# A tile's scatters wait, besides its slots, for the cross query products of the tile two behind it

## Chip, cores, metric

The kernel runs on one core of a Trainium2 chip. The metric is the device time of one execution in microseconds (us); lower is better. The engines are named as in the profile: PE (TensorE), PEld (its weight loads), DVE (VectorE), ACT (ScalarE), POOL (GpSimd) and SP (SyncE).

## What is computed

One decoder layer over 32 sequences of 128 tokens with 512 features: causal self attention with rotary positions, cross attention to a context with int8-like rounding, and a mixture of 64 experts. What is rounded, and what the experts take, is the part that matters here:

```python
def _qdq(x):
    s = jnp.maximum(jnp.max(jnp.abs(x), axis=-1, keepdims=True) / 127.0, 1e-08)
    return jnp.clip(jnp.round(x / s), -127.0, 127.0) * s
...
q = _qdq(x) @ _qdq(wq).T + bq                    # cross query products
...
out = _qdq(o) @ _qdq(wp).T + bp                  # cross attention's output
...
pos = (jnp.cumsum(onehot, axis=0) * onehot).sum(-1) - 1
valid = pos < CAP
dest = jnp.where(valid, slot_expert * CAP + pos, E * CAP)
buf = jnp.zeros((E * CAP + 1, h), xf.dtype).at[dest].set(xf[slot_token])
...
x = x + _L0_attn_ref(_layernorm(x, axis=-1), ...)
x = x + _L0_xattn_ref(_layernorm(x, axis=-1), ctx_2048, ...)
x = x + _L0_ffn_ref(_layernorm(x, axis=-1), ...)
```

Each token goes to 8 of the 64 experts, and each expert takes at most 128 tokens, in the order of the tokens. A token that comes too late for an expert is left out of it.

## The kernel before

**Two stages.** First all 32 sequences pass through both attentions and the router; one sequence of 128 tokens is one tile. Each tile's normed rows are written to a buffer in HBM, `routed`, at the slots of their experts. Then, once all rows are there, the 64 experts run one after the other. The change touches the first stage alone.

**A software pipeline written out by hand.** Each engine runs its own list of steps in its own program order, and `body(cur)` is one pass of it: `Fori(7, B + 1)` makes 26 such passes, and the passes before and behind it are written out. In one pass five tiles are under way at different steps: queries, keys and values of tile `cur - 1`, self attention of `cur - 2`, the cross queries and scores of `cur - 3`, the end of the cross attention of `cur - 4`, and the routing of `cur - 5`. An engine never goes past a step that waits: whatever stands behind it in its list waits as well. Steps of different engines meet through semaphores; `reached(eng, semaphore, m, per, j)` makes an engine wait until the j-th of a tile's `per` signals has come for tile m.

**POOL's list in one pass**, in order: `ctx_hi` (L1829) and `ctx_lo` (L1836), which split the context of tile `cur - 3` in two parts for PE; between them `bias_first_sum` (L1832); `number_tokens` (L1843); `cross_power`, `turned_x_hi`, `turned_x_lo`, `self_power`; then `scatter(cur - 5)` (L1867), then `ffn_power(cur - 4)` (L1822) and `bias_residual(cur - 2)` (L1877). `scatter` issues eight indirect DMAs of 128 rows, one for each of a token's eight experts; rows without a place are skipped. It waits for `d_r2`, DVE's signal that the slot numbers are ready (the last instruction of `slot_numbers` is at L1424).

**The steps around it.** On DVE `find_slots` is followed at once by the cross attention's norm and rounding of tile `cur - 3`. On PE `cross_queries(cur - 3)` multiplies the rounded rows with the rounded weights (`project_int8`, L534, semaphore `p_cq`; `cross_output` shares the line). It stands just behind `turn_probs_1` (`turn_probs`, L556, semaphore `p_pT`). ACT picks both up: `copy_probs_1` (L1022 into `probsT`), then `scale_cross_queries` (L1124 into `cq`, a part of `wide_b`). PE turns the scaled queries (L510 on `wide_b`), multiplies `cross_output` (DVE's `second_sum`, L1384, takes it), turns the probabilities 2 and 0, and makes `cross_scores` (L549) and `turn_probs_3`. DVE's `cross_max_0` and `cross_max_1` (L1341) take the scores, `ffn_rsqrt` (L1318 to L1322, L1481) takes POOL's `ffn_power`, and behind it stand `cross_max_2`, `cross_max_3`, `att_lo`, `rotate` and `first_sum`. ACT's `copy_probs_3` takes `turn_probs_3`, then come `cross_exp_0` and `att_hi` (L1022 into `attT_hi`); PE needs `att_hi` for the products `output_b` and `output_a` (L528 on `w_o`).

Of the kernel before, what the change touches and what calls it, by code (L numbers as in the profile page):

```python
# [66 lines left out]
def nth(ordinal, per, j):  # L67

    return (ordinal - 1) * per + j


def until(eng, semaphore, value):

    if not isinstance(value, int) or value > 0:
        eng.wait_ge(semaphore, value)
# [7 lines left out]
def reached(eng, semaphore, m, per, j):  # L83

    if isinstance(m, int):
        if m < 1:
            return
        m = min(m, B)
    until(eng, semaphore, nth(m, per, j))
# [7 lines left out]
def apart(eng):  # L97


    eng.nop(nofuse=True)  # L100


def layer(nc, x, xT_in, ctxT_in, qT_w, kT_w, vT_w, oT_w, xkT_w, xvT_w, xq_w, xp_w, biases, vb, xkb, xvb, ob, xbq, xbp, routerT,
# [7 lines left out]
    def sem(name):  # L111
        return st.enter_context(nc.semaphore(name))

    with st:
# [89 lines left out]
        def spare(m):  # L204

            return isinstance(m, int) and m == B - 1

        def row_of(m):

            return empty_row if spare(m) else row  # L210
# [5 lines left out]
        def slots_of(m):  # L216

            return slots_spare if spare(m) else slots
# [40 lines left out]
        p_q8T, p_cq, p_cqT = sem("pe_xq8T"), sem("pe_cq"), sem("pe_cqT")  # L259
# [1559 lines left out]
        def _(pool):  # L1819
# [42 lines left out]

            def scatter(m, first=0, end=TOPK):
                reached(pool, d_r2, m, 6, 6)
                apart(pool)
                for k in range(first, end):
                    pool.indirect_dma_start(routed, bass.IndirectOffsetOnAxis(ap=slots_of(m)[:, k:k + 1], axis=0), row_of(m)[:, :], None,  # L1867
                                            bounds_check=SLOTS - 1,
                                            oob_is_err=False).then_inc(s_scatter_spare if spare(m) else s_scatter, 16)
# [9 lines left out]
            def body(cur, split=True):  # L1879
                if has(cur - 3):  # L1880
                    ctx_hi(cur - 3)
                if has(cur - 4):
                    bias_first_sum(cur - 4)
                if has(cur - 3):
                    ctx_lo(cur - 3)
                if has(cur - 5):
                    number_tokens(cur - 5)
                if has(cur - 3):
                    cross_power(cur - 3)
                if has(cur - 1) and split:  # L1890
                    turned_x_hi(cur - 1)
                if has(cur - 1) and split:
                    turned_x_lo(cur - 1)
                if has(cur - 1):
                    self_power(cur - 1)
                if has(cur - 5):
                    scatter(cur - 5)
                if has(cur - 4):
                    ffn_power(cur - 4)
                if has(cur - 2):  # L1900
                    bias_residual(cur - 2)
# [33 lines left out]
            number_tokens(B - 1)  # L1935
            number_tokens(B)
            scatter(B - 1, 0, 2)
            ffn_power(B)
            scatter(B - 1, 2, TOPK)
            scatter(B)  # L1940
            pool.wait_ge(s_scatter, 16 * TOPK * (B - 1))
# [69 lines left out]
```

## Time and profile before

| | |
|---|---|
| median of 3 runs | 1680.09 us (1678.44 to 1685.43) |
| the profiled execution | 1680.71 us, its span 1678.9 us |
| busy share of the span | PE 85%, DVE 71%, PEld 64%, ACT 56%, POOL 43% |
| mean granted TensorE clock | 0.938 of full speed |

A timeline row gives the start, the duration, the engine, the source line, the operation, what it writes and reads, and how many instructions are merged in the row; in brackets stands the engine's idle time before it and what ended it. `remote` there means that the wait ended on a signal that the profile can't put down to an instruction that had just finished. A row of the waits gives the total, the number of times and the longest.

### The profile page before, as it was taken

To read this page: it belongs to the slowest core of one execution; us is meant where nothing else is said; L and a number is where in the kernel's file an instruction comes from. 1 tells how busy PE (TensorE), PEld (TensorE's weight loads), DVE (VectorE), ACT (ScalarE), POOL (GpSimd) and SP (SyncE) were. 2 spreads that over 40 slices of the span, in tenths; PEclk is the share of its full clock that TensorE was granted. 3 is DMA by queue.
4 is the path that set the end of the run, shared out by engine and by line. 5 is a ranking of instruction groups with operands and counts; after the bars stand their busy time and mean duration, and the time that the engine had idled before them with its cause. 6 is when DMAs were issued, how large, how long until landed. Compare 5 with 4: busy or idle time off the path is not lost.

```text
span 1678.9 us, 36380 instructions
## 1 busy us (share of the span) xinstructions
PE 1421.1 (85%) x11243; PEld 1069.3 (64%) x11276; DVE 1189.6 (71%) x3054; ACT 940.6 (56%) x3309; POOL 727.1 (43%) x718
## 2 busy tenths in 40 slices
PE   5499889999988999889899999989864888888895
PEld 3377667777666777666677777767643655555564
DVE  3778878888887888888788888888862444444453
ACT  2367676676666666666666766666742333333342
POOL 1113434444443444445444344444433454445565
PEclk8699999999999999999999999999976999999997
DMA  6765322222211111111111001110464999999964
GB/s 187 296 220 205 136 94 100 92 92 95 100 46 36 38 32 31 31 56 32 31 38 31 31 31 56 31 31 26 161 227 153 282 280 276 279 263 282 280 103 52
DMA packets 164530, 204.33 MB, mean 122 GB/s; under 512 B 40246, under 2 KB 122422, under 8 KB 164481
## 3 DMA queue, kind: packets, MB, share of 16 engines
q1 hardware_dynamic: 125568, 165.86, 30.0%
q0 software_dynamic: 38912, 37.87, 11.1%
q8 instruction: 24, 0.39, 0.1%
q14 instruction: 26, 0.21, 0.0%
HBM read 136.19 MB, written 130.29 MB: 159 GB/s over the span
## 4 chain that ended last, share of the span: by engine, by line
PE 37%; DMA 19%; issue 12%; ACT 10%; DVE 8%; another core or an unknown queue 7%; POOL 1%; POOLq 0%; DVEq 0%; SPq 0%
DMA out<-x,slots 19%; PE bank L528 18%; ACT probs L1028 7%; PE bank L556 6%; PE bank L510 3%; PE bank L563 3%; PE bank L534 2%; PE bank L549 2%; PE bank L569 1%; ACT wide_b L1124 1%; ACT wide_b L1099 1%; DVE small L1308 1%; DVE small L1341 1%; POOL routed L1867 1%
## 5 line engine op out<-in xcount | busy, mean ns | idle before, releaser
L1028 ACT ACTIVATE probs<-bank,small 128x128 f32<-128x128 f32 x1024 | 363.5, 389 | 88.1 <-issue 50.0
L1867 POOL DMA_INDIRECT routed<-row,slots x248 | 253.7, 1023 | 126.7 <-issue 77.4
L1822 POOL TENSOR_TENSOR small<-small,half 128x1 f32<-128x1 f32 x96 | 54.4, 567 | 544.5 <-DVE small L1313 544.5
L1950 POOL DMA_INDIRECT out<-x,slots x128 | 199.0, 1554 | 195.8 <-DMA out<-x,slots 148.4
L1022 ACT ACTIVATE probsT<-bank 128x512 f32<-128x512 f32 x254 | 144.2, 609 | 214.4 <-remote 116.3
L1028 ACT ACTIVATION_READ_ACCUMULATOR probs<-bank,small 128x1 f32 x1024 | 234.6, 229 | 0.0
L1341 DVE TENSOR_REDUCE small<-bank 128x4 f32<-128x512 f32 x256 | 166.4, 682 | 23.0 <-PE bank L549 17.6
L556 PE MATMUL bank<-idf,probs 128*128 128x128 f32 x1024 | 164.8, 300 | 8.5 <-ACT probs L1028 8.4
L556 PEld LDWEIGHTS bank<-idf,probs 128*128 128x128 f32 x1024 | 134.1, 156 | 42.0 <-ACT probs L1028 13.2
L1777 DVE TENSOR_SCALAR slots<-pairs 128x1 uint32<-128x1 f32 x128 | 13.7, 149 | 184.0 <-DMA out<-x,slots 180.3
L1271 ACT ACTIVATE xn<-bank 128x192 f32<-128x192 f32 x64 | 21.3, 333 | 148.2 <-PE bank L968 133.0
L1384 DVE SCALAR_TENSOR_TENSOR x<-bank,small,xp_row 128x512 f32<-128x512 f32 x32 | 24.0, 751 | 110.1 <-PE bank L534 105.7
L968 PE MATMUL bank<-w_gate_up,x_in 128*128 128x384 f32 x256 | 96.0, 522 | 0.5 <-issue 0.5
L1350 DVE TENSOR_TENSOR probs<-probs,small 128x512 f32<-128x512 f32 x128 | 88.8, 693 | 4.4
L968 PE MATMUL bank<-w_gate_up,x_res 128*128 128x384 f32 x256 | 91.3, 501 | 0.0
L510 PE MATMUL bank<-idf,wide_b 128*128 128x128 f32 x128 | 23.1, 309 | 76.9 <-ACT wide_b L1124 76.9
L510 PEld LDWEIGHTS bank<-idf,wide_b 128*128 128x128 f32 x128 | 14.8, 149 | 89.1 <-ACT wide_b L1124 88.7
L968 PEld LDWEIGHTS bank<-w_gate_up,x_in 128*128 128x128 f32 x256 | 49.6, 204 | 30.5 <-issue 7.7
L968 PEld LDWEIGHTS bank<-w_gate_up,x_res 128*128 128x128 f32 x256 | 47.7, 196 | 27.2 <-issue 3.3
L528 PE MATMUL bank<-w_q_hi,xT_hi 128*128 128x512 f32 x128 | 57.8, 451 | 7.8 <-issue 7.8
L528 PE MATMUL bank<-w_o_hi,attT_hi 128*128 128x512 f32 x132 | 54.5, 413 | 11.6 <-DVE attT_lo L1697 10.6
L1783 DVE TENSOR_SCALAR x<-bank,pairs 128x256 f32<-128x256 f32 x128 | 55.5, 476 | 0.0
(250 smaller groups left out, 3974.5 us busy)
## 6 DMA issues: line engine op xcount, KB each, us to landing
w_gate_up<-in_w_gate SPq DMA_DIRECT2D x128, 192.0 KB
w_gate_up<-in_w_up SPq DMA_DIRECT2D x128, 192.0 KB
w_down<-in_w_down SPq DMA_DIRECT2D x128, 192.0 KB
routed<-empty_row SPq DMA_DIRECT2D x16, 1280.0 KB, 11.3
x_in<-in_x SPq DMA_DIRECT2D x32, 256.0 KB
xn<-in_xT_in SPq DMA_DIRECT2D x32, 256.0 KB
ctx_sb<-in_ctxT_in SPq DMA_DIRECT2D x32, 256.0 KB
x_res<-in_x SPq DMA_DIRECT2D x32, 256.0 KB
```

Of the source, the lines that this page charges most:

```text
L510: last = pe.transpose(bank[:, b, t * P:(t + 1) * P], src[:, t * P:(t + 1) * P], idf[:, :])
L528: done = pe.matmul(bank[:, b, :], lhsT, rhs, start=first and k == 0, stop=last and k == len(steps) - 1)
L556: last = pe.transpose(bank[:, b, j * P:(j + 1) * P], probs[:, g, j * P:(j + 1) * P], idf[:, :])
L968: last = pe.matmul(bank[:, 2 + k % 2, 0:2 * F], rowsT[k % 2][:, t * P:(t + 1) * P], w_gu[k][:, :, t, :], start=(t == 0), stop=(t == KT - 1))
L1022: act.activation(dst, src, ACT.Copy).then_inc(done, 1)
L1028: last = act.activation(probs[:, g, j * P:(j + 1) * P], bank[:, b, j * P:(j + 1) * P], ACT.Exp, bias=negated[:, h:h + 1], **({"accum_out": ...
L1341: dve.tensor_reduce(negated[:, g * GH:(g + 1) * GH], bank[:, b, :].rearrange("p (j k) -> p j k", j=GH), AX_X, ALU.max, negate=True).then_i ...
L1350: dve.tensor_tensor(heads, heads, own.unsqueeze(2).to_broadcast([P, GH, P]), ALU.mult).then_inc(d_norm, 1)
L1783: last = dve.tensor_scalar(scaled_y[k % 2][:, cols], bank[:, half_bank(c, k), cols], share[k % NROWS], None, ALU.mult)
L1822: pool.tensor_tensor(c["r0"], c["v"], half[:, :], ALU.pow).then_inc(g_pow[kind], 1)
L1867: pool.indirect_dma_start(routed, bass.IndirectOffsetOnAxis(ap=slots_of(m)[:, k:k + 1], axis=0), row_of(m)[:, :], None, bounds_check=SLOTS ...
L1950: pool.indirect_dma_start(out.rearrange("b p (h c) -> (b p h) c", h=2), bass.IndirectOffsetOnAxis(ap=place_of[k % 2][:, half_:half_ + 1], ...
```

## The change

One line is added to POOL's `scatter`:

```diff
             def scatter(m, first=0, end=TOPK):
                 reached(pool, d_r2, m, 6, 6)
+                reached(pool, p_cq, m + 2, 1, 1)
                 apart(pool)
                 for k in range(first, end):
```

`scatter` is called with `m = cur - 5`, so the new wait is for the cross query products of tile `cur - 3`: those that PE makes in the same pass. For the last tiles the tile number is cut to 32, whose products are there by then. No work is added or taken away.

## Rows read from the trace of the kernel before

**Rows 1.** The waits: engine, what, releaser; us in total, times, longest.

```profile
ACT probsT L1022 <- remote: 116.3, 26, 4.6
```

**Rows 2.** Timeline of PE in two passes.

```profile
721.07 0.66 PE L556 MATMUL bank<-idf,probs 128*128 128x128 f32 x4
721.78 0.81 PE L534 MATMUL bank<-xq_wT,xq8T 128*128 128x512 bf16 x3
...
728.13 0.65 PE L510 MATMUL bank<-idf,wide_b 128*128 128x128 f32 x4 [2.90 <-ACT wide_b L1124]
...
759.01 0.81 PE L534 MATMUL bank<-xq_wT,xq8T 128*128 128x512 bf16 x3
```

**Rows 3.** Timeline of ACT in the same passes.

```profile
726.90 0.60 ACT L1022 ACTIVATE probsT<-bank 128x512 f32<-128x512 f32 x1 [4.48 <-remote]
...
736.76 0.60 ACT L1022 ACTIVATE attT_hi<-bank 128x512 fp32r<-128x512 f32 x1
...
772.44 0.61 ACT L1022 ACTIVATE attT_hi<-bank 128x512 fp32r<-128x512 f32 x1
```

**Rows 4.** Timeline of POOL: scatters of several passes, and what follows in one.

```profile
162.78 1.25 POOL L1867 DMA_INDIRECT routed<-row,slots  x1 [1.56 <-issue]
...
715.21 1.09 POOL L1867 DMA_INDIRECT routed<-row,slots  x1 [1.38 <-DVE chosen_before L1424]
...
724.54 0.98 POOL L1867 DMA_INDIRECT routed<-row,slots  x1 [0.30 <-issue]
...
752.44 1.10 POOL L1867 DMA_INDIRECT routed<-row,slots  x1 [1.38 <-DVE chosen_before L1424]
...
770.46 0.57 POOL L1822 TENSOR_TENSOR small<-small,half 128x1 f32<-128x1 f32 x1 [7.72 <-DVE small L1313]
...
787.92 1.10 POOL L1867 DMA_INDIRECT routed<-row,slots  x1 [1.38 <-DVE chosen_before L1424]
...
1156.26 1.10 POOL L1867 DMA_INDIRECT routed<-row,slots  x1 [1.38 <-DVE chosen_before L1424]
```

**Rows 5.** Timeline of DVE in the same passes.

```profile
714.16 0.19 DVE L1424 TENSOR_TENSOR chosen_before<-chosen_before,chosen 128x64 bf16<-128x64 bf16 x1
...
735.40 0.27 DVE L1318 TENSOR_SCALAR small<-small 128x1 f32<-128x1 f32 x1
...
771.53 0.27 DVE L1318 TENSOR_SCALAR small<-small 128x1 f32<-128x1 f32 x1
```

**Rows 6.** Two stretches by window; behind POOL's count stands the granted clock.

```profile
729.48:732.89 3.41, 3.41 (x13) 2.70 (x11) 2.86 (x6) 2.85 (x10) 0.00 (x0) 0.50 0.15 59
...
1210.76:1214.17 3.41, 2.84 (x7) 2.26 (x8) 3.37 (x4) 2.92 (x13) 2.45 (x3) 0.50 0.00 0
```

**Rows 7.** The pass at 1198 to 1213 us: POOL, PE, ACT and DVE.

```profile
1199.80 0.97 POOL L1867 DMA_INDIRECT routed<-row,slots  x1 [6.22 <-issue]
...
1207.03 0.97 POOL L1867 DMA_INDIRECT routed<-row,slots  x1 [0.30 <-issue]
...
1198.96 0.81 PE L534 MATMUL bank<-xq_wT,xq8T 128*128 128x512 bf16 x3
...
1205.04 0.66 PE L556 MATMUL bank<-idf,probs 128*128 128x128 f32 x4
...
1208.80 0.60 ACT L1022 ACTIVATE probsT<-bank 128x512 f32<-128x512 f32 x1 [3.93 <-remote]
...
1210.66 0.62 ACT L1022 ACTIVATE attT_hi<-bank 128x512 fp32r<-128x512 f32 x1
...
1207.96 1.39 DVE L1341 TENSOR_REDUCE small<-bank 128x4 f32<-128x512 f32 x2 [2.29 <-remote]
...
1209.75 3.13 DVE L1322 TENSOR_TENSOR small<-small 128x1 f32<-128x1 f32 x1
```

**Rows 8.** The pass at 677 to 693 us: POOL and DVE.

```profile
682.70 0.99 POOL L1867 DMA_INDIRECT routed<-row,slots  x1 [4.10 <-issue]
...
693.00 0.75 DVE L1384 SCALAR_TENSOR_TENSOR x<-bank,small,xp_row 128x512 f32<-128x512 f32 x1 [4.41 <-remote]
```

## The prediction, made before the change was run

> **What bounds the kernel now.** I read the page first: PE is busy for 85% of the span, so the question is what its idle time waits for. The waits give one answer that stands out: ACT's copy of turned probabilities waited 26 times, about 4.5 us each, 116.3 us in all [rows 1]. Then I read the timelines of PE, ACT and POOL side by side over one pass. The transposes that this copy waits for ended at 721.07 + 0.66 = 721.73, but ACT started at 726.90 [rows 2, 3]. So PE's result was there 5.2 us before ACT learned of it. POOL's eight scatters run in just this time: the first starts at 715.21, the last ends at 724.54 + 0.98 = 725.52 [rows 4]. ACT is let go 1.38 us after that end. I read this as follows: while POOL issues scatters back to back, PE's signals come late, and they come in a bunch shortly after the last one. The cause inside the chip I can't see; the timing I can.
>
> Through the late signal PE goes idle for 2.90 us [rows 2], and in most passes a stretch at granted clock 0.50 (the 1.2 GHz level) follows at once [rows 6]. A pass with that stretch lasts 752.44 - 715.21 = 37.23 us, one without it 787.92 - 752.44 = 35.48 us, and the mean over 27 passes is (1156.26 - 162.78) / 27 = 36.80 us [rows 4]. So 75% of the passes are long ones ((36.80 - 35.48) / 1.75).
>
> **What the change removes and adds.** Let P be the end of the cross query products: 722.59 in the long pass, 759.82 in the short one [rows 2]. Now the slots are ready 714.16 + 0.19 = 714.35 [rows 5], 8.2 us before P, so the new wait does hold the scatters. `turn_probs_1` and the products themselves then signal with no scatter under way. The 4.5 us wait of the copy goes.
>
> What is late next? I follow one tile from P.
> - P to the first scatter: 715.21 - 714.35 = 0.86 us, what POOL takes now from its releaser to the first scatter [rows 4, 5].
> - Eight scatters: 725.52 - 715.21 = 10.31 us [rows 4].
> - End of the scatters to the late signals: 1.38 us in the pass above, 1208.80 - (1207.03 + 0.97) = 0.80 us in the pass of [rows 7].
> - From the copy of `turn_probs_3` to the end of `att_hi`: 1210.66 + 0.62 - 1208.80 = 2.48 us [rows 7].
>
> So `att_hi`, on which PE's output products hang, ends 14.45 to 15.03 us after P. Today it ends 736.76 + 0.60 - 722.59 = 14.77 us after P in a long pass and 772.44 + 0.61 - 759.82 = 13.23 us in a short one [rows 2, 3]; with 75% long passes that is 14.39 us. The direct cost is 0.06 to 0.64 us a tile; I take 0.3, between the two release times.
>
> Why do I believe that `turn_probs_3` will be held? The trace of before holds one pass in which scatters start right at P: products end at 1198.96 + 0.81 = 1199.77, six scatters start at 1199.80. `turn_probs_3` ended at 1205.70, ACT took it at 1208.80 after 3.93 us of waiting, and DVE's first cross maxima waited 2.29 us as well [rows 7]. After the change every pass looks like this, with eight scatters in place of six.
>
> Two costs come on top.
> - **The clock.** In the pass of [rows 7] PE had little to do from the cross scores until `att_hi`, and the clock then fell to 0.50 for 3.41 us, right in the output products [rows 6]. Today's drop lies ahead of `att_hi` and is inside the 14.77. A drop behind it costs between 0 (DVE's chain is late anyway) and 1.75 us (the difference of a long and a short pass). I take half, 0.9: behind `att_hi` both PE's products and DVE's `att_lo`, `rotate` and `first_sum` stand in front of the next pass, and no row tells which ends last then.
> - **DVE beside POOL.** `ffn_power` stands behind the scatters on POOL, so DVE's `ffn_rsqrt` now runs just as POOL does `bias_residual`, `ctx_hi`, `bias_first_sum` and `ctx_lo` without a break. In the pass of [rows 7] the tiny L1322 took 3.13 us there; its neighbour L1318 of the same size takes 0.27 [rows 5]. That is 0 to 2.86 us a tile; I take 0.4, since it is spent on DVE, beside PE's drop, and the rows show one such case.
>
> The Trainium skill speaks against the change here: GPSIMD Engine Reference, Key points, says that GpSimd shares its SBUF interfaces with VectorE, which contends in instructions with two SBUF inputs, as L1322 is one. The 3.13 us agrees. The page gives no price, so the sum by it would hold this term with an unknown size; the sum by the row holds at most 2.86 us.
>
> What else is queued behind the wait: `ffn_power`, `bias_residual` and the next pass's `ctx_hi`. POOL waits 7.72 us ahead of `ffn_power` today [rows 4], which is nearly all the delay of 0.86 + 8.2 us. No SP load waits for a step that is newly held. The added wait itself is an instruction or two on a POOL that is idle then: nothing.
>
> **The sum.** 0.3 + 0.9 + 0.4 = 1.6 us a tile. 27 passes from 162.78 to 1156.26 are hit; the pass behind them has its scatters there already, and the expert stage is untouched. 27 x 1.6 = 43 us. On the profiled execution's 1680.7 us that is **1724 us**; the median of the runs is 0.6 us lower, which I neglect. Bounds: 27 x 0.06 = 2 us below, and 27 x (0.64 + 1.75 + 0.4) = 75 us above, 1682 to 1756. If the whole 2.86 us of L1322 were to show, it would take the place of the clock's cost and give 27 x (0.64 + 2.86) = 95 us; I count that as unlikely.
>
> **Rivals.**
> - *Faster: PE's signals get through, and POOL alone sets the pace.* It needs `turn_probs_3` and the cross scores to signal within about the first half of the scatters. Then DVE's `ffn_rsqrt` still waits for `ffn_power`: P + 0.86 + 10.31 + (771.53 - 770.46 = 1.07) = P + 12.24 us [rows 4, 5]. In a short pass it starts at P + 11.71, and the rest of a short pass is 35.48 - 11.71 = 23.77 us. The pass becomes 36.01 us, 0.79 less than the mean; 27 x 0.79 = 21 us, 1659 us. For it: the held signals of [rows 7] come 5.24 us and more behind the first scatter (1205.04 against 1199.80), and those of [rows 2] 5.9 us behind it, so steps that are quicker than this could get ahead of the hold. Against it: in [rows 7] the steps were not quicker, with the same work in front of them.
> - *Far slower: `cross_output` is held too.* In the pass of [rows 8] POOL paused 4.10 us after its first scatter, the rest ran later than usual, and `second_sum` waited 4.41 us for `remote`. If each tile pays that: 27 x 4.41 = 119 us, 1800 us. Against it: `cross_output` stands on PE ahead of the cross scores, so it signals earlier than 5.24 us into the scatters.
> - *No change.* The wait of the copy is replaced by one of equal length, and the clock drop costs what it does today: 27 x 0.06 = 2 us, 1682 us.
> - *The wait does nothing.* Excluded by the 8.2 us above.
>
> **How the numbers follow.** Forecast (slower, 1724 us) 0.70; faster 0.18; no change 0.07; far slower 0.05. The range leaves out the far slower case and a part of the ends: 1658 to 1756 us. The forecast's own range is 1682 to 1756. A measurement of this kernel tells about 0.5% (8 us) from no change: slower 0.73 (the forecast without its low end, and the far slower case), same 0.09, faster 0.18.
>
> **What would show it.** In the changed kernel's timeline the copy behind `turn_probs_1` should wait under 1 us for PE; the first scatter should start about 0.9 us after the cross query products; ACT's copy into `probsT` ahead of `cross_exp_0`, or DVE's L1341 on the cross scores, should wait for `remote` until about 1 us after the last scatter; stretches at 0.50 should start behind that wait; and the pass should last about 38.4 us. If none of these waits is there and the pass lasts 36 us, the first rival is right. If L1384 waits for `remote`, it is the second. I would be wrong at the root if PE's signals were late with no scatter under way.

## The result, and the profile after

The changed kernel takes 1767.00 us in the median of three runs (1763.18 to 1767.14), the kernel before 1679.26 us beside it: a ratio of 1.0508, with a 95% interval of 1.0471 to 1.0546. A fourth run of the changed kernel, at 3395.22 us a slow one, is left out. The change is slower, by 88 us in place of the forecast 43, and 11 us above the upper end of the range. The direction and the signs by which I wanted to know the mechanism are there; the size is not.

The waits of the changed kernel come first (engine, line waited for: us in all, times, longest):

```profile
POOL routed L1868 <- PE bank L534: 279.1, 29, 12.9
ACT probsT L1022 <- remote: 189.4, 28, 7.2
...
DVE small L1341 <- remote: 154.7, 29, 6.5
```

The scatters now wait for the cross query products (the first row). The row `probsT <- remote` of [rows 1] stands here again under the same name, but grown from 116.3 us in 26 waits to 189.4 us in 28, and it is another copy: the one of `turn_probs_3`. DVE's maxima of the cross scores wait in the same way. One pass shows it (timelines; start, us, engine, operation, and in brackets the idle time before it with what ended that):

```profile
758.09 0.81 PE L534 MATMUL bank<-xq_wT,xq8T 128*128 128x512 bf16 x3
...
764.34 1.17 PE L549 MATMUL bank<-wide_b 32*128 32x128 f32 x32
765.44 0.66 PE L556 MATMUL bank<-idf,probs 128*128 128x128 f32 x4
...
772.36 1.51 PE L563 MATMUL bank<-probsT,v_sb 128*32 128x128 f32 x24 [4.18 <-ACT probsT L1022]
...
781.81 1.00 PE L569 MATMUL bank<-router_w,x3T 128*128 128x64 f32 x8
...
758.54 0.67 ACT L1022 ACTIVATE probsT<-bank 128x512 f32<-128x512 f32 x1
...
771.71 0.60 ACT L1022 ACTIVATE probsT<-bank 128x512 f32<-128x512 f32 x1 [6.83 <-remote]
...
773.93 0.60 ACT L1022 ACTIVATE attT_hi<-bank 128x512 fp32r<-128x512 f32 x1 [0.18 <-PE bank L563]
...
759.75 1.10 POOL L1868 DMA_INDIRECT routed<-row,slots  x1 [9.51 <-PE bank L534]
...
769.35 0.97 POOL L1868 DMA_INDIRECT routed<-row,slots  x1 [0.30 <-issue]
770.33 0.59 POOL L1822 TENSOR_TENSOR small<-small,half 128x1 f32<-128x1 f32 x1
...
773.89 1.27 POOL L1836 TENSOR_TENSOR cT_lo<-ctx_sb,cT_hi 128x512 fp32r<-128x512 f32 x1
...
771.53 1.29 DVE L1341 TENSOR_REDUCE small<-bank 128x4 f32<-128x512 f32 x2 [5.42 <-remote]
...
773.22 1.96 DVE L1322 TENSOR_TENSOR small<-small 128x1 f32<-128x1 f32 x1
...
782.04 0.68 DVE L1506 TENSOR_TENSOR x<-bank,x_res 128x512 f32<-128x512 f32 x1
782.86 0.22 DVE L1510 TENSOR_REDUCE small<-bank 128x1 f32<-128x64 f32 x1
```

The copy behind `turn_probs_1` (758.54) no longer waits: the 4.48 us of [rows 3] are gone. The cross scores ended at 764.34 + 1.17 = 765.51 and `turn_probs_3` at 766.10, but DVE and ACT learned of it at 771.53 and 771.71, just over 1 us behind the end of the last scatter (769.35 + 0.97 = 770.32). `ffn_power`, for which POOL waited 7.72 us in [rows 4], follows the scatters at once. Behind the stall the clock is at its lower level, as in [rows 6], but now in the attention and value products (windows; us, then busy time of PE, PEld, DVE, ACT and POOL, then granted clock, DMA share and GB/s):

```profile
772.41:773.80 1.39, 1.39 (x25) 0.94 (x25) 1.32 (x4) 1.34 (x8) 1.39 (x2) 0.50 0.00 0
773.80:777.21 3.41, 3.41 (x12) 2.71 (x9) 3.37 (x6) 3.27 (x15) 1.72 (x3) 0.53 0.00 0
```

To see where the time lies I take the starts of `router_max` (L1510), one in each pass. After:

```profile
191.91 0.22 DVE L1510 TENSOR_REDUCE small<-bank 128x1 f32<-128x64 f32 x1 [0.58 <-PE bank L569]
...
1253.36 0.22 DVE L1510 TENSOR_REDUCE small<-bank 128x1 f32<-128x64 f32 x1 [0.58 <-PE bank L569]
...
1333.52 0.20 DVE L1510 TENSOR_REDUCE small<-bank 128x1 f32<-128x64 f32 x1
```

Before, the same three, and two from the middle that are used further down:

```profile
189.58 0.23 DVE L1510 TENSOR_REDUCE small<-bank 128x1 f32<-128x64 f32 x1
...
744.43 0.21 DVE L1510 TENSOR_REDUCE small<-bank 128x1 f32<-128x64 f32 x1
...
779.91 0.23 DVE L1510 TENSOR_REDUCE small<-bank 128x1 f32<-128x64 f32 x1
...
1184.29 0.22 DVE L1510 TENSOR_REDUCE small<-bank 128x1 f32<-128x64 f32 x1
...
1251.81 0.20 DVE L1510 TENSOR_REDUCE small<-bank 128x1 f32<-128x64 f32 x1
```

Between the first two rows lie 27 passes: (1253.36 - 191.91) / 27 = 39.31 us each, against (1184.29 - 189.58) / 27 = 36.84 us. That is 27 x 2.47 = 66.7 us. The two passes up to the last of these rows take 80.16 against 67.52 us: 12.6 us more. Ahead of them the span has grown by 191.91 - 189.58 = 2.3 us, behind them by 0.8 us. The sum, 82.4 us, is the difference of the spans (1761.4 and 1678.9 us); the profiled run is the quickest of the three, so it shows 82 of the 88 us.

### The profile page after: what moved, and what is told of

Same layout as the page of the kernel before. It is cut to its first block, busy times and chain, and to the rows that moved or that the text cites. A ratio compares the mean times of both kernels' runs of the same rounds, so it can differ in the third digit from the quotient of the medians.

```text
span 1761.4 us, 36380 instructions
## 1 busy us (share of the span) xinstructions
PE 1453.7 (83%) x11243; PEld 1088.9 (62%) x11276; DVE 1221.3 (69%) x3054; ACT 943.9 (54%) x3309; POOL 730.9 (41%) x718
## 4 chain that ended last, share of the span: by engine, by line
DVE 31%; DMA 18%; PE 16%; issue 15%; another core or an unknown queue 10%; ACT 4%; POOL 2%; DVEq 1%; POOLq 0%; SPq 0%
DMA out<-x,slots 18%; PE bank L528 10%; DVE small L1341 4%; DVE small L1308 3%; DVE small L1331 2%; DVE small L1322 2%; DVE chosen L1405 2%; PE bank L563 1%; ACT probs L1028 1%; POOL routed L1868 1%; PE bank L556 1%; ACT probsT L1022 1%; DVE wide_a L1377 1%; ACT wide_b L1137 1%
## 5 line engine op out<-in xcount | busy, mean ns | idle before, releaser
L1868 POOL DMA_INDIRECT routed<-row,slots x248 | 258.0, 1040 | 366.0 <-PE bank L534 279.1
L1341 DVE TENSOR_REDUCE small<-bank 128x4 f32<-128x512 f32 x256 | 166.5, 682 | 162.7 <-remote 154.7
L1022 ACT ACTIVATE probsT<-bank 128x512 f32<-128x512 f32 x254 | 145.2, 617 | 231.0 <-remote 189.4
L1028 ACT ACTIVATION_READ_ACCUMULATOR probs<-bank,small 128x1 f32 x1024 | 228.0, 223 | 0.0
L563 PE MATMUL bank<-probsT,v_sb 128*32 128x128 f32 x1024 | 74.4, 374 | 115.5 <-ACT probsT L1022 96.0
L556 PE MATMUL bank<-idf,probs 128*128 128x128 f32 x1024 | 150.2, 280 | 14.5 <-ACT probs L1028 11.0
L556 PEld LDWEIGHTS bank<-idf,probs 128*128 128x128 f32 x1024 | 119.1, 143 | 45.1 <-ACT probs L1028 17.0
L563 PEld LDWEIGHTS bank<-probsT,v_sb 128*32 128x32 f32 x1024 | 41.2, 145 | 146.3 <-ACT probsT L1022 108.9
L528 PE MATMUL bank<-w_v_hi,xT_hi 128*128 128x512 f32 x128 | 75.6, 591 | 0.0
L1322 DVE TENSOR_TENSOR small<-small 128x1 f32<-128x1 f32 x96 | 69.7, 726 | 3.3
L528 PE MATMUL bank<-w_v_lo,xT_hi 128*128 128x512 f32 x128 | 68.8, 537 | 0.4 <-issue 0.4
```

The source lines that it names most:

```text
L528: done = pe.matmul(bank[:, b, :], lhsT, rhs, start=first and k == 0, stop=last and k == len(steps) - 1)
L556: last = pe.transpose(bank[:, b, j * P:(j + 1) * P], probs[:, g, j * P:(j + 1) * P], idf[:, :])
L563: last = pe.matmul(bank[i * DH:(i + 1) * DH, b, g * P:(g + 1) * P], values[:, h * DH:(h + 1) * DH], probsT[:, g, i * P:(i + 1) * P], start ...
L1022: act.activation(dst, src, ACT.Copy).then_inc(done, 1)
L1028: last = act.activation(probs[:, g, j * P:(j + 1) * P], bank[:, b, j * P:(j + 1) * P], ACT.Exp, bias=negated[:, h:h + 1], **({"accum_out": ...
L1322: dve.tensor_tensor(c["r"], c["u"], c["r0"], ALU.mult).then_inc(s, 1)
```

## The experiments

Theory A, from the prediction: scatters that POOL issues back to back hold PE's signals, and the added wait moves the hold from `turn_probs_1` to the cross scores and `turn_probs_3`. Rival B: POOL's own order (`ffn_power` behind the scatters) sets the pace. Rival C: the late signals belong to a place in PE's program. Rival D: the low clock behind the stall is the larger part. All ratios below are to the kernel before on the same chip; "a pass" is the mean of the 27 passes as above, in the profiled run. Before it is 36.84 us, after the change 39.31. Of each edit the lines that matter are shown.

### Four scatters in place of eight, before and after

```diff
-                for k in range(first, end):
+                for k in range(first, min(end, 4)):
```

> The kernel before with four of eight scatters for each tile; the rows of places 5 to 8 are left out, so the output lacks their shares. A: the run ends 5.1 us after its start, ahead of the end of turn_probs_1, so the copy no longer waits 4.5 us, 1530 to 1600 us. B: POOL waits 7.7 us ahead of ffn_power already, so shorter scatters bring nothing: 1680 us. C: 1680 us.

> The changed kernel with four of eight scatters for each tile; the rows of places 5 to 8 are left out, so the output lacks their shares. A: the run ends at P + 6.0 us and the cross scores end at P + 7.2 us, so the waits of 6.8 us (copy into probsT) and 5.4 us (L1341) vanish, a pass lasts 32 to 35 us, 1550 to 1630 us. B: ffn_power comes 5.1 us sooner, at most 27 x 5.1 = 139 us less than 1763, if all of that shows; half of it gives 1690. C: 1763 us, as POOL is not part of it.

Measured: 1535.60 us without the added wait (ratio 0.9118, 0.9094 to 0.9142; a pass 32.06 us) and 1543.79 us with it (0.9164, 0.9138 to 0.9189; a pass 32.01 us). Of the waits for `remote` only single ones are left, where the kernel before had 26 and the changed one 28 and 29. C falls. The hold costs the kernel before 36.84 - 32.06 = 4.8 us a pass, and with runs this short the added wait costs nothing a pass; the 8 us between the two kernels lie in the last passes.

### POOL as busy as before, but no scatter

```diff
-                for k in range(first, end):
-                    pool.indirect_dma_start(routed, ...
+                for k in range(18):
+                    if k >= 7:
+                        reached(pool, s_scatter, m, 18, k - 6)
+                    pool.tensor_tensor(filler[:, 1 + k % 7:2 + k % 7], filler[:, 0:1], filler[:, 0:1],
+                                       ALU.pow).then_inc(s_scatter, 1)
```

> The changed kernel with no scatter at all: at their place POOL runs 18 small powers, one like ffn_power each, which take it about as long (10 to 12 us) but move nothing by DMA. All rows for the experts are left out, so the output lacks the experts' part; the expert stage itself does the same work on empty rows. A: no signal of PE is held, the waits behind the cross scores are under 1 us; what stays is that ffn_power comes at P + 11 to P + 13 us, a pass of 34 to 37 us, 1600 to 1700 us. B: POOL is occupied as long as before in the same place, so the time stays at 1740 to 1765 us. C: the same as B, and the waits behind the cross scores stay at 5 to 7 us.

Measured: 1655.18 us (0.9835, 0.9811 to 0.9859), a pass 35.71 us. A pass of it:

```profile
703.33 10.86 POOL L1871 TENSOR_TENSOR filler<-filler 128x1 f32<-128x1 f32 x18 [9.51 <-PE bank L534]
...
710.13 1.29 DVE L1341 TENSOR_REDUCE small<-bank 128x4 f32<-128x512 f32 x2
714.74 0.27 DVE L1318 TENSOR_SCALAR small<-small 128x1 f32<-128x1 f32 x1 [3.32 <-POOL small L1822]
```

POOL works for 10.86 us, but L1341 starts without a wait: it is the scatters that hold PE's signals, not a busy POOL. What is left is B's part: `ffn_rsqrt` waits 3.32 us for `ffn_power`, and a pass costs 35.71 - 32.06 = 3.65 us more than with nothing in its way. This is the pass of my first rival (36.01 us) almost to the number. Whether the changed kernel would last as long with its scatters and no hold, this kernel can't tell: without scatters L1322 behind `ffn_power` lasts 0.74 us in the median, and with them far longer, as the next kernel shows.

### The later place

```diff
-                reached(pool, p_cq, m + 2, 1, 1)
+                reached(pool, p_xs, m + 2, 4, 4)
```

> The changed kernel with its added wait put 7.2 us further on: on the last of the cross scores in place of the cross query products. A: the cross scores and turn_probs_3 signal with no scatter under way, so the waits of 6.8 and 5.4 us go; the hold then falls on what ends about 14 to 20 us behind P, the output products above all. POOL's ffn_power comes 7.3 us later than in the changed kernel. If the place of the hold alone counts: 1650 to 1750 us. If POOL's order counts as much as the filler showed (3.65 us a pass when ffn_power came at P + 11.7): a pass of 42 to 44 us, 1840 to 1890 us. If both: above 1767 us, with first_sum or router_max waiting for remote.

Measured: 1939.39 us (1.1613, 1.1585 to 1.1641), a pass 45.31 us: slower than the range for either mechanism alone, and without the sign of both, as neither `first_sum` nor `router_max` waits for `remote`. The waits, then one pass:

```profile
DVE small L1318 <- POOL small L1822: 260.8, 29, 12.6
```

```profile
770.57 0.60 ACT L1022 ACTIVATE attT_hi<-bank 128x512 fp32r<-128x512 f32 x1 [3.87 <-remote]
...
775.51 0.27 DVE L1318 TENSOR_SCALAR small<-small 128x1 f32<-128x1 f32 x1 [9.76 <-POOL small L1822]
...
776.01 3.72 DVE L1322 TENSOR_TENSOR small<-small 128x1 f32<-128x1 f32 x1
```

The hold now sits on `att_hi`, but `att_hi` is done at 771.17, 4.3 us before `ffn_rsqrt` gets what it waits for. What sets this pass is B: `ffn_rsqrt` waits 9 us for POOL, and then L1322 lasts 3.72 us, until POOL's `ctx_lo` ends. In the median of its passes L1322 ends at P + 22.44 us, `router_max` starts 7.47 us later and the next P comes 15.31 us behind that: 45.2 us, the whole pass.

### Two runs of four

```diff
                 for k in range(first, end):
+                    if k == 4:
+                        reached(pool, p_cq, m + 2, 1, 1)
+                        apart(pool)
```

> The kernel before, with the eight scatters of a tile cut into two runs: four at the slots, as before, then the added wait for the cross query products, then the other four. Theory A (scatters issued back to back hold PE's signals, from about 5 us into a run until 1.3 us after its end; the added wait only moves the hold to later signals): each run lasts 5.1 us, so hardly a signal is held; the 4.5 us wait of the copy behind turn_probs_1 and the 5 to 7 us waits behind the cross scores are both under 1.5 us, a pass lasts 32 to 35 us, and the time is 1540 to 1620 us, under both kernels. Theory B (what stands behind the scatters on POOL, ffn_power above all, sets the pace): ffn_power comes at P + 6 us, where its input is just there, so nothing is late: 1660 to 1680 us. Theory C (the late signals belong to a place in PE's program and not to the scatters): the copy waits as before, 1680 us or above.

Measured: 1571.52 us (0.9328, 0.9298 to 0.9357), a pass 32.80 us. The same wait that makes the kernel slower ahead of all eight scatters makes it 6.7% faster ahead of the second four.

The other split seemed as good:

```diff
-                if has(cur - 5):
-                    scatter(cur - 5)
+                if has(cur - 5):
+                    scatter(cur - 5, 0, 4)
                 if has(cur - 4):
                     ffn_power(cur - 4)
+                if has(cur - 5):
+                    scatter(cur - 5, 4, TOPK)
```

> The kernel before with the scatters cut into two runs without any added wait on PE: four at the slots, then ffn_power, which waits for DVE's statistics anyhow, then the other four. A: no run is longer than 5.1 us, so the copy behind turn_probs_1 and the copies behind the cross scores wait under 1.5 us; a pass of 32 to 34 us, 1535 to 1600 us. The other four end about 6 us behind ffn_power, and ffn_normed has to wait for them: if that ends last, up to 2 us more a pass, 1600 to 1650 us. B, with C: ffn_power no later than before, nothing else changed, 1680 us.

Measured: 1676.35 us (1.0042, 1.0027 to 1.0056), a pass 36.77 us. A missed, although no run is longer than 5 us:

```profile
766.95 1.08 PE L563 MATMUL bank<-probsT,v_sb 128*32 128x128 f32 x32
...
773.32 0.50 PE L528 MATMUL bank<-w_o_hi,attT_hi 128*128 128x512 f32 x1 [3.23 <-ACT attT_hi L1022]
...
772.67 0.60 ACT L1022 ACTIVATE attT_hi<-bank 128x512 fp32r<-128x512 f32 x1 [4.37 <-remote]
...
766.98 1.04 POOL L1867 DMA_INDIRECT routed<-row,slots  x1 [0.21 <-issue]
```

The second run starts at 766.98, the attention products end at 768.03, only 1 us into it, and ACT learns of it at 772.67. So "free for the first 5 us" was wrong. What differs here is how much PE does in that first microsecond: some 34 matmuls.

### A short pause

```diff
+                    if k == 4:
+                        for j in range(2):
+                            pool.tensor_tensor(filler[:, 1 + j:2 + j], filler[:, 0:1], filler[:, 0:1],
+                                               ALU.pow).then_inc(s_fill, 1)
+                        reached(pool, s_fill, m, 2, 2)
```

> The changed kernel with two small powers on POOL (about 1.1 us) between the fourth and the fifth scatter. If the hold comes of unbroken issue and a short pause ends it: the waits of 6.8 and 5.4 us behind the cross scores fall under 1.5 us, and what stays is ffn_power behind the scatters, at P + 12.3 us, a pass of about 36 us as with the filler in place of the scatters, 1655 to 1695 us. If the hold goes by how much POOL issued in the last 10 us or so, and the pause is too short: the waits get longer by 1.1 us, 1767 + 27 x 1.1 = 1797 us.

> The kernel before with two small powers on POOL (about 1.1 us) between the fourth and the fifth scatter, no wait on PE. N, with a count that starts anew behind a short pause: turn_probs_1, cross queries and turn_quantised_o fall into the second run of four as its first 15 or so matmuls, so nothing that counts is held: 1560 to 1610 us. If the pause of 1.1 us is too short to start the count anew: held as before and POOL is 2 us later, 1690 to 1740 us. T, with the time counted from the end of the pause: 1560 to 1610 us also.

Measured in the changed kernel: 1808.36 us (1.0841, 1.0815 to 1.0866), a pass 40.87 us; in the kernel before: 1566.23 us (0.9391, 0.9366 to 0.9416), a pass 32.63 us. In the changed kernel the time is that of "too short", but the rows are those of the other case:

```profile
788.00 1.11 POOL L1873 TENSOR_TENSOR filler<-filler 128x1 f32<-128x1 f32 x2
...
788.86 1.29 DVE L1343 TENSOR_REDUCE small<-bank 128x4 f32<-128x512 f32 x2
...
788.92 0.60 ACT L1024 ACTIVATE probsT<-bank 128x512 f32<-128x512 f32 x1 [1.24 <-PE bank L558]
...
794.17 0.60 ACT L1024 ACTIVATE attT_hi<-bank 128x512 fp32r<-128x512 f32 x1 [3.08 <-remote]
```

(Its lines stand two further down.) POOL works 1.1 us in the pause, and from the fourth scatter's end to the fifth's start 1.98 us pass. That frees the cross scores and `turn_probs_3`; the second run of four then holds the attention products. But this hold is not what makes the pass long: `att_hi` ends at 794.77, 13.08 us behind the end of the cross query products (P, 781.69), and in the changed kernel 15.63 us behind it. DVE does:

```profile
795.49 0.27 DVE L1320 TENSOR_SCALAR small<-small 128x1 f32<-128x1 f32 x1 [5.34 <-issue]
...
795.99 3.75 DVE L1324 TENSOR_TENSOR small<-small 128x1 f32<-128x1 f32 x1
```

`ffn_power` starts at P + 13.18 us in the median, 1.76 us later than in the changed kernel, `ffn_rsqrt` stands for it (here until 795.45), and its third instruction again lasts until `ctx_lo` ends (P + 18.0). From there `router_max` is 7.47 us away, as above, in all 27 passes right behind DVE's own chain. Freeing the scores gained nothing: the expectation missed because it took over the 36 us of the kernel without scatters, and with them POOL's order alone, pause included, makes 40.8.

### Time or number?

To see what sets in the hold, the end of each PE matmul that signals is put beside the moment at which the trace has the signal: the k-th signal of a semaphore beside the k-th matmul that sends it. A few matmuls have no record, so a count can be one or two short. The matmuls are counted from the first scatter of an unbroken run of eight (in the third column, of the second run of four). Each entry: how many signals, where in the run the middle four fifths of them lie (us), their median delay (us).

```
matmul of the run   before               after                four, power, four    wait for the scores
1 to 15             21, 2.2, 0.01        110, 0.1-2.0, 0.01   57, 0.0-0.4, 0.04    54, 0.5-0.9, 0.03
16 to 20            none                 20, 2.8, 0.01        25, 0.6-0.7, 1.42    27, 1.1, 0.92
21 to 26            24, 5.1, 0.77        52, 3.3-3.7, 0.01    29, 0.8, 3.35        1, 1.2, 0.21
27 to 30            26, 6.0, 4.14        19, 4.4-4.7, 0.01    none                 26, 1.3, 2.15
31 to 35            55, 6.5-7.4, 4.39    none                 29, 1.0-1.2, 4.62    27, 1.5-1.6, 4.11
36 and more         86, 8.3-10.0, 2.82   188, 5.7-7.9, 6.05   56, 2.1-3.1, 3.08    120, 2.7-9.5, 3.56
```

By time the rows contradict each other: 4.7 us into a run signals are free in the changed kernel, and 0.6 us into one they are late in the kernel split at `ffn_power`. By number they agree at both ends: up to the 15th free, from the 31st on late. Between these, number alone does not tell either: the 16th to 20th are free where they end 2.8 us into the run, and late where they come at 0.6 to 1.1 us. Held signals come in order, and some of them while the run goes on: in the last column those of the 31st to 35th come 5.7 us into a run that lasts 10. A reading found in the same rows that it explains has to be tried, so I added matmuls on PE that bring more of them early in the run:

```diff
                 reached(pe, e_xkT, m, 1, 1)
+                for k in range(24):
+                    pe.matmul(bank[0:DH, 0, 0:DH], cT_hi[:, k % KT, 0:DH], W["xv"][0][:, k % KT, 0:DH], start=True, stop=True)
                 project(0, cT_hi, cT_lo, "xv", 1, True, False).then_inc(p_xv, 1)
```

> The kernel before with 24 tiny matmuls (32 by 32) on PE ahead of cross_values_b, just behind the start of the scatters; they write a corner of a bank that the next matmul overwrites, so they add nothing to the result. The question is what sets in the hold: theory T (time: signals are free for about 5 us of a run) or theory N (number: about 30 matmuls of PE get through in an unbroken run of scatters, however long they take, and the signals of later ones are held). T: the added matmuls cost PE about 0.8 us a pass and the copy behind turn_probs_1 is held as before: 1675 to 1710 us. N: the 30 are used up before turn_quantised_x, whose signal is then held until about 1 us after the eighth scatter, 8 to 9 us; the copy of xq8T waits for it, the cross query products come late, and with them all behind: 1780 to 1940 us.

Measured: 1771.89 us (1.0650, 1.0606 to 1.0694), a pass 39.71 us: 8 us short of the bound given for N, far outside that for T. One wait, and one pass, where the first scatter started at 795.32:

```profile
ACT xq8T L1024 <- remote: 160.1, 27, 7.6
```

```profile
795.56 0.99 PE L625 MATMUL bank<-w_xv_hi,cT_hi 128*32 128x32 f32 x24
...
797.41 0.40 PE L515 MATMUL bank<-idb,xq 128*128 128x128 bf16 x4
...
804.00 0.60 ACT L1024 ACTIVATE xq8T<-bank 128x512 bf16<-128x512 bf16 x1 [4.76 <-remote]
...
804.65 0.98 POOL L1869 DMA_INDIRECT routed<-row,slots  x1 [0.30 <-issue]
```

`turn_quantised_x` (L515) ended at 797.81, 2.5 us into the run, and the copy of `xq8T`, which never waits for `remote` in the kernel before, came at 804.00. That is before the eighth scatter began (804.65), and not behind the run as expected. The 24 added were 32 wide, as were the products in all early holds so far, so the kind was still open:

```diff
-                    pe.matmul(bank[0:DH, 0, 0:DH], cT_hi[:, k % KT, 0:DH], W["xv"][0][:, k % KT, 0:DH], start=True, stop=True)
+                    pe.matmul(bank[:, 0, 0:DH], cT_hi[:, k % KT, :], W["xv"][0][:, k % KT, 0:DH], start=True, stop=True)
```

> As the kernel with 24 tiny matmuls, but each of the 24 uses a full 128 by 128 weight tile (and still 32 columns of data), so that no 32-wide product stands among the first matmuls of the scatters; they add nothing to the result either. The early holds seen so far all had 32-wide products in them (attention products, cross scores, the 24 tiny ones), so the kind could set in the hold and not the number. N (number): xq8T waits for remote in nearly every pass, about 160 us in all, as with the tiny ones, a pass of 39 to 41 us, 1750 to 1800 us. K (kind): turn_quantised_x signals freely, xq8T waits under 1 us, and the copy behind turn_probs_1 is held as in the kernel before: 1680 to 1730 us with the 1 to 2 us that the added matmuls take of PE.

Measured: 1754.22 us (1.0509, 1.0422 to 1.0596), a pass 39.21 us.

```profile
ACT xq8T L1024 <- remote: 159.6, 25, 7.6
```

So added matmuls bring the hold forward with full weights too. In this run they took longer, and `turn_quantised_x` ended 4.2 to 5.5 us into the run; its median delay was 5.27 us, where the signals at 5.1 us in the kernel before had 0.77. Time alone is out by the tiny ones, and narrow weights by these. How fast the matmuls come may count beside their number, by the table; no run changes the pace alone, and what sets in the hold stays open to that extent.

### Five and three

```diff
-                    if k == 4:
+                    if k == 5:
                         reached(pool, p_cq, m + 2, 1, 1)
```

> As the kernel split at the cross query products, but with five scatters at the slots and three behind the wait. N: turn_probs_1 is about the 27th to 30th matmul from the start of the first run (6.4 us), on the edge; the second run (3.8 us) holds only 21 to 25 matmuls, so the 1.2 us by which queries_c was held there and the 0.4 us of the cross scores go. If the edge holds: 1550 to 1570 us. If turn_probs_1 is held to the end of the first run, it costs up to 1.3 us a pass: 1570 to 1605 us. T: the first run is over 5 us long, so turn_probs_1 is held, 1590 to 1605 us.

Measured: 1555.80 us (0.9330, 0.9303 to 0.9356), a pass 32.24 us, and without the one in which POOL paused 4.53 us (37.3 us) all are 31.8 to 32.4: the pass of the kernel with four scatters, with all eight done.

```profile
720.81 0.97 POOL L1870 DMA_INDIRECT routed<-row,slots  x1 [1.76 <-PE bank L534]
...
719.82 0.60 ACT L1022 ACTIVATE probsT<-bank 128x512 f32<-128x512 f32 x1
...
727.13 1.29 DVE L1341 TENSOR_REDUCE small<-bank 128x4 f32<-128x512 f32 x2
```

Between the fifth scatter and the sixth POOL stands for 1.76 us (the first row). Neither the copy nor the maxima wait. By the ratio it is no better than four and four (the intervals cover each other), by the pass it is 0.6 us better.

### The clock by itself

```diff
                 weigh_turned(3, 1, v_sb, p_pv)
+                for k in range(0 if isinstance(m, int) and m >= B else 32):
+                    pe.matmul(bank[:, 3, 3 * P:4 * P], xT_hi[:, k % KT, :], W["v"][0][:, k % KT, 0:P], start=True, stop=True)
```

> The changed kernel with 32 more matmuls of 128 by 128 on PE behind the first eight attention products, at the place where PE stands idle for 4.2 us; they write a part of the bank that the next products overwrite, so they add nothing to the result. They do not shorten any hold. Theory D (the low clock behind the idle stretch is a cost of its own, 1.31 us a tile behind att_hi and 0.65 us in the 24 attention products): the clock stays at 1.0, a pass lasts 37.3 to 38.2 us in place of 39.3, and the time is 1705 to 1735 us. Theory A without D (the low clock lies beside other work): 1755 to 1775 us. If the added matmuls take more than the idle stretch, it would be above 1767 us.

Measured: 1874.29 us (1.1237, 1.1211 to 1.1264), a pass 42.84 us. The matmuls that were to fill the idle stretch did not run in it:

```profile
746.53 0.66 PE L702 MATMUL bank<-w_v_hi,xT_hi 128*128 128x128 f32 x4
747.76 0.57 PE L702 MATMUL bank<-w_v_hi,xT_hi 128*128 128x128 f32 x4 [0.56 <-issue]
749.19 4.78 PE L702 MATMUL bank<-w_v_hi,xT_hi 128*128 128x128 f32 x24 [0.86 <-issue]
```

After eight of them PE itself stood, with its operands there; the other 24 came at 749.19, just over 1 us behind the end of the last scatter, and took 4.78 us of their own. D is not tested by this and stays open as a separate cause: in the hold PE can't be kept busy. What the low clock takes, the rows below don't part from the rest either.

## Why the prediction was right in its sign and wrong in its size

**What bounds the kernel before, and where the hold goes: right.** Scatters hold PE's signals; the wait of [rows 1] moved from `turn_probs_1` to `turn_probs_3` and the cross scores; the changed pass looks like that of [rows 7]. The kernels with four scatters and with the powers show that the scatters hold the signals. That the hold alone sets the changed kernel's pass was wrong: three steps of the sum failed.

**First step, the direct cost: the term was 0.3 us and measured 1.24.** In the pass shown, P is 758.09 + 0.81 = 758.90. First scatter at P + 0.85 (forecast 0.86); the eight take 770.32 - 759.75 = 10.57 us (10.31); the release comes 771.71 - 770.32 = 1.39 us later (0.80 to 1.38); from there to the end of `att_hi`, 773.93 + 0.60, are 2.82 us (2.48). So `att_hi` ends at P + 15.63, where I had 14.45 to 15.03, and today's mean was 14.39. Every link came out at its long end or just beyond. I took the release from the middle of two passes, and the 2.48 us from one pass; here the 24 attention products alone took 1.51 us at clock 0.50.

**Second step, what lies behind `att_hi`: 0.9 for the clock and 0.4 for L1322 forecast, 1.31 measured for all of it.** From the end of `att_hi` to `router_max` are now 782.86 - 774.53 = 8.33 us. Before they were 744.43 - 737.36 = 7.07 us in the long pass and 779.91 - 773.05 = 6.86 in the short one, 7.02 in the mean of [rows 4]'s shares. The two terms add up to what was measured, but not for the reason given. I took L1322's time as spent beside PE's drop. In the pass shown PE's logits end at 782.81 and DVE's `first_sum` at 782.72, with DVE at work without a pause from 771.53. In 14 of the 27 passes `router_max` starts straight behind `first_sum`, mostly some 0.45 us after the logits; in the other 13 it waits for the logits. So two chains of nearly equal length set the pass: the hold, `att_hi` and PE's products at the lower clock; and POOL's `ffn_power` behind the scatters, L1322 and DVE's chain. Taking away one alone would leave most of the cost, and the share of the clock stays open.

L1322 lasts until POOL's `ctx_lo` ends: 773.22 + 1.96 = 775.18, against 773.89 + 1.27 = 775.16; in the two kernels above it lasted 3.7 us, to the same point. That VectorE instructions with two SBUF inputs contend with GpSimd the Trainium skill says in GPSIMD Engine Reference, Key points. These rows agree: further on in the same pass, with POOL idle, L1322 took 0.16 us. By this second chain alone, in the medians, the pass is 16.27 (P to the end of L1322) + 7.47 + 15.29 = 39.03 us.

From `router_max` to the next P (its products end at 798.15) nothing changed (15.29 us, before 15.39). So a pass costs 1.24 + 1.31 - 0.10 = 2.45 us more, against 1.6 forecast; the mean says 2.47.

**Third step, the number of passes: 27 forecast, 29 held (the first row of the waits).** I left out the passes at the ends, "the pass behind them has its scatters there already". The last two cost 12.6 us. In one of them POOL paused within its run, and `ffn_power` stood behind it:

```profile
1276.50 0.98 POOL L1868 DMA_INDIRECT routed<-row,slots  x1 [5.63 <-issue]
...
1284.51 0.27 DVE L1318 TENSOR_SCALAR small<-small 128x1 f32<-128x1 f32 x1 [10.01 <-POOL small L1822]
```

The kernel before has such a pause too (ahead of 1199.80 in [rows 7]), but there POOL is some 7.7 us early in other passes, and it was hidden. I had written that this slack is used up, and costed it at nothing. It should have had the price of a pause that is no longer covered. This step put the time outside the range: 27 x 2.47 = 66.7 us alone would have given 1747 us, inside it.

**The rivals.** The faster one was right on POOL where there are no scatters (35.71 us a pass, 36.01 forecast) and failed on its condition: the cross scores are about the 30th to 62nd matmul of the run. My argument for it was the time from the first scatter, and that alone is not what counts. It also took L1322 as short: with the scores free and scatters ahead (the kernel with the pause) POOL's order made a pass of 40.8 us; without the 1.76 us of the pause that is, as an estimate, 39.0 us, so even with its condition met this rival would not have been faster. `cross_output` (the far slower one) ends as about the 17th, and in the changed kernel L1384 has no wait for `remote`: its condition failed by the same count. The wait did what it says (279.1 us of waiting).

**The range** left too little above the sum: it joined the long ends of two terms, but with one number of passes and no pause.

## What to carry to other kernels

When a wait for `remote` stands on a producer that ended long ago, look at what another engine issues in just that time, and count before you move it: a hold does not go away by coming later, it falls on whatever signals then, and what stands behind the moved work on its engine comes later too. Break up a long run of scatters, with a wait or a pause of two microseconds, so that each piece covers few matmuls; here that was worth 6 to 7%, with the very wait that cost 5% ahead of all of them. And an engine's slack is a cover: if a change uses it up, the rare long pause gets a price.

## What the runs showed of the hardware that was not expected

- In an unbroken run of scatters the signals of PE's first 15 matmuls come freely and those from the 31st on late (0.01 to 0.04 us and 2.8 to 6.1 us in the medians of the four kernels of the table). Between these it varies: free 2.8 us into a run, 1.42 us late 0.6 us into one. Held signals come in order, most of them soon after the run's end, some within it. Where POOL paused 2.0 us between two scatters, the signals behind the pause got through (1566.23 us in place of some 1667).
- Held long enough, PE itself stops: 0.56 and 0.86 us with its work at hand, in the kernel with the added products. What in the chip does this is open; the runs show the delays, not the part.
- A 128x1 instruction of DVE (L1322) lasted 3.7 us, across several instructions of POOL that followed without a break, and ended with the last of them but one, `ctx_lo`.
- POOL paused 2.96 us and 5.63 us between two scatters of one run in the changed kernel, and nothing in the trace releases it. The pass with the first took 41.5 us in place of 39.3. The pauses are not by chance: in all eleven kernels with eight scatters a tile they stand ahead of the 114th and the 227th scatter (2.9 to 6.5 us), in the two with four ahead of the 114th.
